# An encoder with chunked linear attention: new layout of the output banks, a bank taken between two half masks, and GpSimd's row adds and W1 part moved

## What is computed

```python
q, k, v = heads(x @ Wq + bq), heads(x @ Wk + bk), heads(x @ Wv + bv)
A = tril(phi(q) @ phi(k).T)                # in a chunk of 128 tokens, per head
num = A @ v + phi(q) @ KV                  # KV: sum over the chunks before
den = A @ 1 + phi(q) @ z + EPS
x = layer_norm(x + (num / den) @ Wo + bo)
x = layer_norm(x + gelu(x @ W1 + b1) @ W2 + b2)
```

## Time and profile before

| | us |
|---|---|
| median of 3 runs | 1674.86 (1674.7 to 1677.55) |
| the profiled execution, its own time | 1675.59 |
| its span | 1673.9 |
| busy: TensorE / its weight loads | 1499.6 / 1190.7 |
| busy: VectorE | 1453.8 |
| busy: ScalarE / GpSimd | 915.5 / 868.6 |

### The profile page before, as it was taken

The page is one execution under the profiler, slowest core; times in us unless marked ns, Lnnn a source line. Parts: engine busy times, 40 slices in busy tenths (PEclk is TensorE's granted clock), DMA queues, the critical chain, the costliest instruction groups (busy, mean ns, idle before and its releaser), DMA issues.

```text
span 1673.9 us, 37828 instructions
## 1 busy us (share of the span) xinstructions
PE 1499.6 (90%) x15318; PEld 1190.7 (71%) x15318; DVE 1453.8 (87%) x2856; ACT 915.5 (55%) x1468; POOL 868.6 (52%) x626
## 2 busy tenths in 40 slices
PE   4699899898998989999899999989988899999898
PEld 4587778777787777888777877778877566666434
DVE  4989999999999999999999999999896788888456
ACT  3355455564455554555545556455534677777445
POOL 4254546546455454554555645555456366664334
PEclk8899999999999999999999999999999899999999
DMA  7120011200111011210012100110105344442001
GB/s 131 35 62 14 20 23 35 62 14 21 24 38 59 14 20 24 57 46 8 21 23 63 41 7 20 24 39 19 30 16 138 119 139 151 137 133 78 15 0 51
DMA packets 99022, 82.48 MB, mean 49 GB/s; under 512 B 23712, under 2 KB 87072, under 8 KB 98848
## 3 DMA queue, kind: packets, MB, share of 16 engines
q1 hardware_dynamic: 98848, 80.06, 18.1%
HBM read 50.78 MB, written 14.68 MB: 39 GB/s over the span
## 4 chain that ended last, share of the span: by engine, by line
DVE 46%; PE 45%; issue 5%; ACT 1%; SPq 1%; DMA 0%; POOL 0%; ACTq 0%; DVEq 0%
DVE e_am L787 11%; DVE e_qx_lo L871 8%; PE e_pr L169 4%; PE e_pr L170 4%; PE e_pr L171 4%; PE x_psO L1351 4%; DVE e_a_blk L805 4%; DVE e_o_blk L797 3%; PE e_sc L169 3%; PE e_sc L171 3%; PE e_sc L170 3%; PE f_bank L1889 3%; PE x_psT L1336 2%; DVE X L744 2%; PE x_psS L1314 2%
## 5 line engine op out<-in xcount | busy, mean ns | idle before, releaser
L701 POOL TENSOR_TENSOR e_h_lo<-e_h_f,e_h_hi 128x512 fp32r<-128x512 f32 x192 | 249.4, 1302 | 278.4 <-ACT e_h_hi L540 275.1
L539 ACT ACTIVATE e_h_f<-e_pr,e_h_bias 128x512 f32<-128x512 f32 x192 | 131.6, 685 | 229.9 <-PE e_pr L171 226.1
L787 DVE TENSOR_TENSOR e_am<-e_sc,c_amask 128x1024 f32<-128x1024 f32 x192 | 223.9, 1205 | 16.0 <-PE e_sc L407 16.0
L1661 DVE TENSOR_REDUCE x_mx<-x_psS 128x4 f32<-128x1024 f32 x128 | 150.9, 1218 | 25.8 <-PE x_psS L1314 24.9
L169 PE MATMUL e_pr<-e_yT_hi,e_W_hi 128*128 128x512 f32 x384 | 172.9, 450 | 0.0
L432 PE MATMUL e_tr<-e_am,e_vx 128*32 128x128 f32 x3072 | 115.5, 296 | 58.1 <-DVE e_o_blk L797 58.1
L169 PE MATMUL e_tr<-e_W_hi,e_h_hi 128*128 128x256 f32 x576 | 163.8, 284 | 1.9 <-DVE X L744 1.9
L170 PE MATMUL e_tr<-e_W_lo,e_h_hi 128*128 128x256 f32 x576 | 161.4, 280 | 0.0
L171 PE MATMUL e_tr<-e_W_hi,e_h_lo 128*128 128x256 f32 x576 | 161.4, 280 | 0.0
L679 POOL TENSOR_TENSOR e_k_lo<-e_qkT,e_k_hi 128x512 fp32r<-128x512 f32 x48 | 67.3, 1421 | 176.7 <-ACT e_k_hi L549 176.7
L170 PE MATMUL e_pr<-e_yT_lo,e_W_hi 128*128 128x512 f32 x384 | 158.5, 413 | 0.0
(11 more groups left out here) (280 smaller groups left out, 4435.4 us busy)
## 6 DMA issues: line engine op xcount, KB each, us to landing
e_raw_m<-in_L_attn_W_dram SPq DMA_DIRECT2D x12, 1024.0 KB, 5.3
x_qs<-query_rows SPq DMA_DIRECT2D x48, 256.0 KB
e_x_raw<-e_x_blk SPq DMA_DIRECT2D x368, 32.0 KB, 1.9
x_ks<-key_rows SPq DMA_DIRECT2D x48, 128.0 KB, 2.7
query_rows<-x_q_hi SPq DMA_DIRECT2D x16, 256.0 KB, 2.1
query_rows<-x_q_lo SPq DMA_DIRECT2D x16, 256.0 KB, 2.3
x_ctok<-in_ctx_dram SPq DMA_DIRECT2D x8, 256.0 KB, 3.3
x_xo<-in_x_dram SPq DMA_DIRECT2D x8, 256.0 KB, 3.5
```

Of the source, the lines that this page charges most:

```text
L539: act.activation(h_f[:, m % HR, :], ps_pr[m % 2][:, :], ACT.Gelu, bias=h_bias[:, m:m + 1])
L701: pool.tensor_tensor(h_lo[:, m, :], h_f[:, m % HR, :], h_hi[:, m, :].bitcast(F32), ALU.subtract).then_inc(h_lo_done, 1)
L787: dve.tensor_tensor(am[:, s % 2, c, :, :, :], ps_sc[:, :, c * 2 * P:(c + 1) * 2 * P].rearrange("p r (h n) -> p r h n", n=P), amask[:, :].u ...
L1661: dve.tensor_reduce(mx[:, N % 2, :, 0:HG].rearrange("p i (a h) -> p h a i", a=2)[:, pair], ps_s[pair][:, :, :].rearrange("p a (i j) -> p a ...
```

## The change

Its parts, in the order of the diff:

- `o_blk`, `a_blk` keep their sizes and get the order (half c, block of 32 tokens b, group g of two in the half) in place of (group, block of 32 tokens). So that a bank can be read in that order, `attend` writes the odd blocks, which lie in one bank, in runs of 32 columns with a step of 64; the even ones lie in two banks as before, and the take alternates between the banks every 32 columns.
- GpSimd: the low part of W1 waits for `qx_lo_done`, the semaphore of the last `qx_lo` of the step. The add of `bo` moves from behind `k_lo` to the end of the step, behind the last `h_lo`, and is for the tile of the step after: tile (q + 2) % 4, once its block transpose (`xT_tr`) is done.
- VectorE: `mask` takes a list of halves; `take`, the first instruction of `divide`, is a function of its own. For s = 0 to 2 it stands between the two halves of `mask(s + 1)`, and for s = 3 right ahead of `divide`, behind `out_lo(2)`.
- The last transposes, two of 128 columns whose source has runs of 16, become one of 256 columns with contiguous source.

```diff
--- before.py
+++ after.py
@@ -93,7 +93,7 @@
     qkT = sb_att("qkT", [2 * KC, TT])
     parity = sb_att("parity", [2])
     ktok = sb_att("ktok", [2, KC, P])
-    o_blk, a_blk, aT_f = sb_att("o_blk", [4, NR, HP]), sb_att("a_blk", [4, NR, DH]), sb_att("aT_f", [KC, P])
+    o_blk, a_blk, aT_f = sb_att("o_blk", [H, HP]), sb_att("a_blk", [H, DH]), sb_att("aT_f", [KC, P])
     den, rden = sb_att("den", [SB, H]), sb_att("rden", [SB, H])
     aT_hi, aT_lo = qx_hi[:, :, 0, :], qx_hi[:, :, 1, :]
     qk_bias_all, qk_bias, qk_bias1 = sb_att("qk_bias_all", [L * 2 * KC]), sb_att("qk_bias", [2 * KC]), sb_att("qk_bias1", [2 * KC])
@@ -409,7 +409,9 @@
                     mm.then_inc(sc_full, 1)
 
                 def out_block(s, g):
-                    return ps_tr2[:, g % 2, blk(g // 2)] if s % 2 == 0 else ps_tr2[:, 0, blk(g)]
+                    if s % 2 == 0:
+                        return ps_tr2[:, g % 2, blk(g // 2)]
+                    return ps_tr2[:, 0, :].rearrange("p (c b g n) -> p c b g n", c=KC, g=2, n=HP)[:, g // 2, :, g % 2, :]
 
                 def attend(s):
 
@@ -682,10 +684,9 @@
                     w_o(1)
                     w_m("W1", w1_hi, 1, w1_lo)
                     x_lo(t + 1)
-                elif attn:
-                    if q == 0 and l > 0:
-                        w_m("W1", w1_hi, l + 1, w1_lo)
-                    add_row(ta, rows_a["bo"], xT_tr, t + 2, bo_loaded, 16 * (la + 1), xbo_done)
+                elif attn and q == 0 and l > 0:
+                    pool.wait_ge(qx_lo_done, t + 1)
+                    w_m("W1", w1_hi, l + 1, w1_lo)
                 if mlp:
                     add_row(q, rows_m["b2"], yT_tr, 2 * u + 2, b2_loaded, 16 * (l + 1), xb2_done)
                     for m in range(FC):
@@ -702,6 +703,9 @@
                                            ALU.subtract).then_inc(h_lo_done, 1)
                         if m == 4 and following:
                             x_lo(t + 1)
+                if following:
+                    ln = l + 1 if q >= NT - 2 else l
+                    add_row((q + 2) % NT, rows_a["bo"], xT_tr, t + 3, bo_loaded, 16 * (ln + 1), xbo_done)
 
             def rsqrt(i, ready, value):
                 pool.wait_ge(ready, value)
@@ -779,36 +783,36 @@
                 def low(out, bank, part):
                     return dve.tensor_tensor(out, bank, part.bitcast(F32), ALU.subtract)
 
-                def mask(s):
+                def mask(s, chunks=range(KC)):
                     dve.wait_ge(sc_full, SB * t + s + 1)
                     if s >= 2:
                         dve.wait_ge(out_full, SB * t + s - 1)
-                    for c in range(KC):
+                    for c in chunks:
                         dve.tensor_tensor(am[:, s % 2, c, :, :, :],
                                           ps_sc[:, :, c * 2 * P:(c + 1) * 2 * P].rearrange("p r (h n) -> p r h n", n=P),
                                           amask[:, :].unsqueeze(1).unsqueeze(1).broadcast_to([P, NR, 2, P]), ALU.mult).then_inc(am_done, 1)
 
-                def divide(s):
+                def take(s):
                     n = SB * t + s
                     dve.wait_ge(out_full, n + 1)
                     wait(dve, den_step, 3 * n)
-                    taken = (ps_tr2[:, :, 0:2 * P].rearrange("p b (j n) -> p j b n", n=P) if s % 2 == 0
+                    taken = (ps_tr2[:, :, 0:2 * P].rearrange("p g (b n) -> p b g n", n=HP) if s % 2 == 0
                              else ps_tr[0][:, :])
-                    dve.transpose(o_blk[:, :, :, :].rearrange("p g b d -> p (g b d)"), taken).then_inc(o_taken, 1)
+                    dve.transpose(o_blk[:, :, :].rearrange("p b d -> p (b d)"), taken).then_inc(o_taken, 1)
+
+                def divide(s):
+                    n = SB * t + s
                     dve.wait_ge(o_taken, n + 1)
-                    o = o_blk[:, :, :, :].rearrange("p g b d -> p (g b) d")
-                    dve.tensor_scalar(den[:, s, :].unsqueeze(2), o[:, :, DH:HX], DEN_EPS, None, ALU.add).then_inc(den_step, 1)
+                    dve.tensor_scalar(den[:, s, :].unsqueeze(2), o_blk[:, :, DH:HX], DEN_EPS, None, ALU.add).then_inc(den_step, 1)
                     dve.wait_ge(den_step, 3 * n + 1)
                     dve.reciprocal(rden[:, s, :], den[:, s, :]).then_inc(den_step, 1)
                     dve.wait_ge(den_step, 3 * n + 2)
                     wait(dve, aT_tr, n)
-                    dve.tensor_tensor(a_blk[:, :, :, :].rearrange("p g b d -> p (g b) d"), o[:, :, 0:DH],
-                                      rden[:, s, :].unsqueeze(2).broadcast_to([P, H, DH]), ALU.mult).then_inc(den_step, 1)
+                    dve.tensor_tensor(a_blk[:, :, :], o_blk[:, :, 0:DH], rden[:, s, :].unsqueeze(2).broadcast_to([P, H, DH]),
+                                      ALU.mult).then_inc(den_step, 1)
                     dve.wait_ge(den_step, 3 * n + 3)
                     wait(dve, aT_lo_done, n)
-                    for c in range(KC):
-                        v = dve.transpose(aT_f[:, c, :], a_blk[:, 2 * c:2 * c + 2].rearrange("p g b d -> p b g d"))
-                    v.then_inc(aT_tr, 1)
+                    dve.transpose(aT_f[:, :, :].rearrange("p c n -> p (c n)"), a_blk[:, :, :].rearrange("p b d -> p (b d)")).then_inc(aT_tr, 1)
 
                 def out_lo(s):
                     dve.wait_ge(aT_hi_done, SB * t + s + 1)
@@ -908,12 +912,16 @@
                     moments(2, d)
                 for s in range(SB):
                     if attn and s + 1 < SB:
-                        mask(s + 1)
+                        mask(s + 1, (0,))
+                        take(s)
+                        mask(s + 1, (1,))
                     if u == final and s == 0:
                         centre(2, d, last, rows_m["g2"], ln2_rows_loaded, rows)
                     if attn:
                         if s > 0:
                             out_lo(s - 1)
+                        if s + 1 == SB:
+                            take(s)
                         divide(s)
                 if u == final:
                     cross.x1_transposed(0, cross.early(1))
```

## The result

| | before | after |
|---|---|---|
| median (lowest to highest), us | 1675.8 (1674.7 to 1677.55), 5 runs | 1659.37 (1655.23 to 1663.14), 5 runs |
| ratio, 95% interval | | 0.9903 (0.9881 to 0.9924) |
| profiled span | 1673.9 | 1657.6 |
| busy VectorE / TensorE | 1453.8 / 1499.6 | 1435.8 / 1491.1 |
| first centring to the end of the last step | 61.4 to 1242.6 = 1181.2 | 63.9 to 1225.4 = 1161.5 |

The change makes the kernel 16.3 us faster (12.7 to 19.9 by the interval). The forecast was 32.5 us faster: right in sign, within the range, and twice too large. The profiled span fell by 16.3 as well: 19.7 gained in the loop, 2.5 lost ahead of it, 0.9 behind it.

The account below looks back on a forecast made before the run. VectorE's chain was taken to set the step, with TensorE close behind. From 1675.6 us, terms of -5 - 7 - 0 - 1 - 14 - 5.5 = -32.5 gave 1643 us, range 1612 to 1672.

Parts of the forecast that it names:

- Parts 1 to 3: GpSimd's edits: W1's wait gains 15 us, `bo` leaving `qx_lo` gains 38, its new place loses 48; together -5.
- Part 4: Last block transposes: one of 256 columns takes 0.43 us against about 0.51 for two, gaining 7 us.
- Part 5: Division, `den`, `rden` and the take in the new tensor order: cost and gain nothing.
- Part 6: TensorE writing odd attention blocks in runs of 32 columns: no cost taken.
- rival E: Attention output of blocks 1 and 3: strided bank writes are dear, giving 1726 us; chance 0.08.
- Part 7: Take between half masks: 1 us gained; TensorE's wait before block 3 shrinks from 2.1 us to about 0.6.
- rival D: Low clock moves from block 3 to the y transposes, 19 of 23 steps losing 1.6 us: +30, 1673; chance 0.12.
- A: The forecast itself for the whole kernel: 1643 us, by itself 1632 to 1656; chance 0.43.
- Part 8: VectorE's `a_blk` collides less with GpSimd's `h_lo`: -0.6 us a step, 14 us; bounds +5 and -30.
- rival C: `a_blk` stays as blocked as it is, the add of `bo` costs 2.4 us, other gains hold: 1661; chance 0.25.
- Part 9: VectorE's waits for the output projection go, as TensorE is 1 to 3 us earlier: -5.5 us.
- part 3: Add of `bo` behind the eighth `h_lo` blocks `e_ve` or the centring: 2.2 us in 22 steps, 48 us lost.

Follow-up runs that it names:

- e2: Changed kernel with GpSimd's old order (W1 not waiting, add of `bo` behind `k_lo`): 1669.62 us, ratio 0.9965.
- e1: Kernel before with only the two GpSimd edits (W1's wait, add of `bo` at the step's end): 1664.98 us, ratio 0.9941.
- e5: Changed kernel with the mask in one piece and the take directly ahead of the rest of `divide`: 1658.66 us, ratio 0.9887.
- e8: Changed kernel with each `k` transpose before the y transposes written four times, filling idle TensorE: 1642.25 us, ratio 0.9793.
- e3: Changed kernel with the add of `bo` behind the last `qx_lo` of its own step, waiting in every step: 1604.12 us, ratio 0.9575.
- e10: e3 with the mask in one piece and the take back inside `divide`: 1626.10 us, ratio 0.9697.
- e13: e5 with each `k` transpose written four times: 1672.20 us, ratio 0.9968.
- e14: e2 with each `k` transpose written four times: 1653.21 us, ratio 0.9855.
- e11: Kernel before with each `k` transpose written four times: 1677.01 us, ratio 1.0005.
- e12: Changed kernel with `e_ve` made by a reduction with one SBUF input in place of an add with two: 1643.68 us, ratio 0.9807.

## Why the prediction was right in sign and twice too large

**Parts 1 to 3 were right in their mechanism.** The undisturbed `e_qx_lo` of 739 ns that they start from stands in this row of the kernel before, as the lowest value:

```profile
L871 DVE SCALAR_TENSOR_TENSOR e_qx_lo<-e_qkT,e_parity,e_qx_hi x2: 739/1810/2881, 738.9 to 741.7; 128x512 fp32r<-128x512 f32 x2
```

W1's wait and the leave of `bo` together took 45.2 us from `e_qx_lo` (forecast 53). `e_ve` took 2.42 us beside an add of 2.40, and `e_ve` and the centring rose by 40.9 less 3.3 (forecast 48). Net -7.6 in the groups, forecast -5. Between e2 and the changed kernel, where GpSimd's edits are the only difference, `e_qx_lo` fell by 53.7, `e_ve` rose by 44.4, and the time fell by 10. That e1 gave 9.9 as well is in part luck: there the groups gave nothing, and the gain was the idle time named above. The cover named for W1 held: its subtractions ran from 681.16 to 686.14, well ahead of the scores of block 1 (695.71). What the forecast did not see is the step ahead of the loop. There the first add, for tile 1, stands at 52.36 to 54.74, beside an `out_lo` that took 1.77 us at 53.26 in place of 0.43, and a take waits 1.31 us for TensorE at 51.51. The loop begins 2.5 us later; with GpSimd's part alone (e1) it was 1.7, with the other part alone (e2) 1.5.

**Part 4 was right**: 96 transposes at 445 ns, 5.7 us (forecast 430 ns and 7 us). **Part 5** as well: the take is at 708 ns, was 704.

**Part 6 was right and rival E is refuted.** TensorE's output of an even and an odd block, after:

```profile
743.80 1.08 PE L434 MATMUL e_tr<-e_am,e_vx 128*32 128x128 f32 x32
747.74 1.08 PE L434 MATMUL e_tr<-e_am,e_vx 128*32 128x128 f32 x32
```

Runs of 32 columns with a step of 64 take the time of one run of 128. Of the two sentences of the Trainium skill (Advanced Engine Details and Errata, "Memory Cachelines") the second, that two consecutive elements are enough, agrees with this row; the first, read alone, does not.

**Part 7 was right about TensorE's wait and wrong in what it summed.** TensorE's wait before block 3 went, and removing it paid nothing (e5 against the changed kernel: 0.0016). The new wait at the take is 6.4 us over the kernel, close to 0.25 x 24 = 6, but by luck: in the 22 steps from 110 us on it is only 2.8, and 3.6 lie ahead of them. What was passed over is what the early take does to the waits of the whole step: part 7 put it at -1 us, and against e5 VectorE's idle time rose by 15.1. As long as VectorE sets the step, TensorE's idle has to go somewhere. Some of it went to the transposes of y (from 34.6 to 39.0 us), more to the scores and to the output projection, and the clock now fell behind y, on VectorE's chain. That is **rival D**, given 0.12 and 30 us, and priced apart from A. It came half true: the low clock stands at y in 9 steps (4 before), and holding the clock up gives 18.4 us (e8). This is one half of the failed step.

**Part 8 is the other half, and the term of the sum that failed.** -14 us was forecast for fewer collisions of `a_blk`. `a_blk` did what was said (under 750 ns: 695, -18.0; in block 1 it starts 0.14 ahead of `h_lo`), but the sum of `a_blk`, `out_lo` and `e_den` stayed at 164.4 us before and after. Against e5 it fell by 3.5, from 167.9; the 14.3 us by which VectorE's busy time fell there lie elsewhere, most of them in the centring (93.9 to 80.6, with `e_ve` up by 5.6), which no part of the forecast has. I looked at the one instruction that was blocked in the timeline and not at what stands next on VectorE when it isn't. The words "as blocked as it is" of **rival C** describe the sum, and its 1661 is close to the 1659.4 measured, but by its own wording (`a_blk` stays, the add costs 2.4) it did not happen: `a_blk` fell and its neighbours rose.

**Part 9 was right where it spoke**: VectorE's wait at the output projection went from 5.5 to 0, and that of the residual adds out of `e_tr` from 9.2 to 1.5. But the one for `e_pr` rose from 13.3 to 17.9, that of `out_lo` for ScalarE from 22.8 to 25.5, and `e_yT_lo`'s from 5.2 to 7.9, the last behind the slower transposes of y: -13.2 and +10.0.

**The sum again**, on VectorE, whose busy time fell by 18.0 while its idle time rose by 1.7: -16.3, the whole difference of the spans. Of the busy time the named groups carry 13.3 (-45.2 + 40.9 - 3.3 - 5.7 + 0); the other 4.7 lie in no one of them, as neighbours overlap in it. Of the idle time, the take brings +6.4, the waits of part 9 -3.2. What the forecast had beyond this is part 8's 14 us, for which no more than 3.5 can be found, and a fall of the idle time by some 6 (parts 7 and 9) that did not come: it rose by 1.7. How much of the 18.4 us that the clock costs is new with the change stays open: the kernel before lost some at y too, but it has no filled twin that reached a clock of 1.00.

The larger price was forecast and accepted as given: the add's new place costs 46.5 us in `e_ve`, as part 3 has it. Behind the last `qx_lo`, where e3 puts it, no group of VectorE is over 3 us longer than in the changed kernel.

## What to carry to other kernels

When an instruction stands still beside another engine's, look for a place where a whole stretch of the victim's queue can't be blocked, and make the other engine wait for it: that gave 55 us here, while shifting starts by tenths of a microsecond only chose another victim. Before you remove an engine's wait, ask which engine sets the step: the same early take was worth nothing where VectorE set it without the take (e5), and 20 and 29 us where TensorE did (e10, e13). And when an engine that isn't the bound is made faster, say where its idle time goes next and what it does to the clock there.

## What the runs showed of the hardware that was not expected

- At the transposes of y, waits of up to 1.9 us came with a granted clock of 0.50 behind them in 9 steps, and twelve repeated transposes a step, which removed these, made the kernel 18.4 us faster (e8; e14 likewise). More work for TensorE was a gain there; on the kernel before it brought nothing (e11), and on e5 it cost 13.6 us (e13), where the low clock stood mostly around block 3 and stayed there.
- A small instruction can be the victim as well as a large one: `e_den`, 16 columns, one SBUF input, took 0.15 us in one place (at 746.69 us) and 1.27 beside GpSimd's subtractions (705.54), and `e_ve`, four columns, 2.42. When one victim was made immune, the next in the queue stood still in its place: of the 46.5 us that the add of `bo` cost `e_ve`, 41.9 came back in the centring (e12).
- A block transpose of 128x256 takes 445 ns, of which two of 128x128 had taken 291 each, overlapping.
